# Attention scores of a decoder layer: three partial passes packed into two full ones and a pair of half-height ones

## The reference

```python
# q: (2, 16 heads, 512 queries, 96), k and v: (2, 4 groups, 1536 keys, 96); 4 heads share a group
scores = jnp.einsum('bkgqd,bksd->bkgqs', q, k) * scale          # scale = 1/sqrt(96)
attn = jax.nn.softmax(scores.astype(jnp.float32), axis=-1)
out = jnp.einsum('bkgqs,bksd->bkgqd', attn, v)
```

## Time and profile before

| | us |
|---|---|
| median of 3 runs | 3467.85 (3467.83 to 3468.65) |
| time of the profiled execution | 3465.8 |
| its span, first to last instruction | 3464.5 |
| PE busy, whole span | 3015.0 (87%) |
| attention, first score matmul to last value matmul | 1661.3 to 2306.1 |
| mean granted TensorE clock, whole span | 0.917 of full speed |

### The profile page before, as it was taken

One profiled execution on the slowest core, in us unless ns is written; L12 is line 12 of the kernel. 1 busy time (PEld: TensorE's weight loads), 2 busy tenths in 40 slices (PEclk: granted clock), 3 DMA queues, 4 the chain that ended last, 5 costly groups with the idle time before them and its releaser, 6 DMA issues. The chain is left out here.

```text
span 3464.5 us, 37038 instructions
## 1 busy us (share of the span) xinstructions
PE 3015.0 (87%) x12731; PEld 2191.7 (63%) x12731; DVE 2160.8 (62%) x1655; ACT 1502.2 (43%) x2400; POOL 1391.3 (40%) x796
## 2 busy tenths in 40 slices
PE   8994567776774799998999999979899999999996
PEld 7861222222231478886788888867688888888884
DVE  5557799999999565401777777764734324324326
ACT  4446355555554443311688888862322112112111
POOL 0003899999999331000688888850100000000001
PEclk9985788887885799999899999989999999999998
DMA  3225865655554474322111111134211101111101
GB/s 139 88 75 209 240 162 125 155 145 149 127 136 114 165 260 166 105 76 92 33 33 51 33 33 37 33 113 147 68 46 53 58 34 53 52 39 54 49 18 61
DMA packets 159386, 331.29 MB, mean 96 GB/s; under 512 B 28221, under 2 KB 40253, under 8 KB 157789
## 3 DMA queue, kind: packets, MB, share of 16 engines
q1 hardware_dynamic: 141694, 320.11, 30.5%
q10 hardware_dynamic: 17568, 9.66, 0.9%
HBM read 257.03 MB, written 72.68 MB: 95 GB/s over the span
## 5 line engine op out<-in xcount | busy, mean ns | idle before, releaser
L731 POOL TENSOR_TENSOR scan_dbx<-scan_u,scan_b_bc 128x1024 f32<-128x1024 f32 x256 | 595.0, 2357 | 25.0 <-DMA scan_u<-u 21.8
L1545 POOL TENSOR_TENSOR at_p_lo<-at_p,at_p_hi 128x512 fp32r<-128x512 f32 x384 | 516.7, 1352 | 148.3 <-ACT at_p_hi L1451 137.2
L918 POOL TENSOR_TENSOR ff_y<-ff_y,ff_rstd 128x512 f32<-128x512 f32 x14 | 24.9, 1806 | 1123.0 <-DVE ff_rstd L907 1123.0
L682 ACT ACTIVATE scan_ps_a<-scan_dt,scan_a_neg 128x512 f32<-128x512 f32 (+1 forms) x512 | 331.7, 680 | 289.8 <-DVE scan_g L694 271.0
L705 DVE TENSOR_TENSOR_SCAN scan_ps_a<-scan_ps_a,scan_dbx 128x1024 f32<-128x1024 f32 x192 | 433.1, 2282 | 7.0 <-ACT scan_ps_a L684 7.0
L792 PE MATMUL scan_ps_y<-scan_g,scan_sel 128*32 128x512 f32 x1024 | 176.2, 765 | 220.8 <-DVE scan_g L694 216.3
L1490 DVE TENSOR_REDUCE at_neg_max<-at_ps_mx 128x1 fp32r<-128x1536 f32 x132 | 232.0, 1758 | 154.4 <-PE at_ps_mx L1565 143.3
L1965 DVE TENSOR_TENSOR ff_hf<-ff_sg,ff_ps_u 128x1024 f32<-128x1024 f32 x28 | 34.2, 1221 | 388.4 <-PE ff_ps_u L98 388.4
L1448 ACT ACTIVATE at_p<-at_ps_s 128x512 f32<-128x512 f32 x384 | 227.9, 593 | 105.2 <-PE at_ps_s L1582 84.2
L1451 ACT ACTIVATE at_p_hi<-at_p 128x512 fp32r<-128x512 f32 x384 | 242.8, 632 | 12.3
L772 PE MATMUL scan_ps_x<-scan_x,scan_wz 128*128 128x512 f32 x448 | 230.0, 661 | 13.5 <-DMA scan_wz<-in_w_in 13.5
(11 more groups left out here) (260 smaller groups left out, 7255.7 us busy)
## 6 DMA issues: line engine op xcount, KB each, us to landing
scan_dt<-dt SPq DMA_DIRECT2D x128, 256.0 KB, 4.6
scan_u<-u SPq DMA_DIRECT2D x128, 256.0 KB, 7.6
ff_w<-in_w SPq DMA_DIRECT2D x56, 512.0 KB, 4.2
mid_w<-in_w_out SPq DMA_DIRECT2D x32, 512.0 KB, 4.7
ff_w<-in_w SPq DMA_DIRECT2D x56, 256.0 KB, 2.6
ff_wo_wo<-in_w_o SPq DMA_DIRECT2D x32, 384.0 KB, 3.1
in_w<-in_w_in SPq DMA_DIRECT2D x18, 512.0 KB, 3.7
xc<-xc SPq DMA_DIRECT2D x16, 512.0 KB, 2.8
```

The source lines that it names most:

```text
L682: nc.scalar.activation(at[:, h * L + h:(h + 1) * L], dt[it % 2][:, c, h:L], ACT.Exp, scale=a_neg[:, it % IT, e:e + 1]).then_inc(a_ready, 1)
L731: nc.gpsimd.tensor_tensor(dbx[n % SL][:].rearrange("p (h l) -> p h l", h=2), u[it % 2][:, c:c + 2], b_bc[:, b, k // 2].unsqueeze(1).to_bro ...
L1545: nc.gpsimd.tensor_tensor(p_lo[t % NSL][:], p[t % NSL][:], f32(p_hi[t % NSL][:]), ALU.subtract).then_inc(p_lo_done, 1)
```

## The change

The three score passes of a tile have 97 + 96 + 96 = 289 rows. The change packs them otherwise: a first pass of 128 rows (`ka`, `qa`: 96 rows high by high, and the first 32 rows of the keys' rest by the queries' high part), a second of 128 rows (`kb`, `qb`: the other 64 rows of the keys' rest, and 64 rows of high by the queries' rest), and a third of 33 rows (`kc`, `qc`: the last 32 rows of high by rest, and the row of maxima). The 33 rows stand twice in `kc` and `qc`, at partitions 0 and 64, and of two key tiles the even one uses rows 0 to 32, the odd one rows 64 to 96.

So that two tiles' third passes stand together, PE works by pairs: two full passes of tile 2j, two of tile 2j+1, then both third passes, then (in j = 5) the transposes, then two tiles of `values`, then, in j = 0 to 3, a maximum of the next head. ACT does two exponentials, then two high parts.

The parts are put in place by DMAs from SBUF to SBUF, which SP issues: five for each head (`stack_q`) and five for each group (`stack_k`). The row of maxima is copied twice: by ACT to partition 96 and by DVE to partition 32 (`row`), for which DVE also copies the column of maxima (`second_column`). The maxima of head 0 use two sets of banks in turn (`ps_first`); keys and values have semaphores of their own; the values of non-existing tiles and the maxima of the non-existing 33rd head are gone.

```diff
-    SPLIT_AT = ((1, 4), (1, 7), (1, 10), (2, 1), (2, 4), (2, 9))
+    SPLIT_AT = ((1, 2), (1, 3), (1, 4), (2, 0), (2, 1), (2, 3))
...
+            def stack_q(hd):
+                s, e = hd % 2, hd % NQ
+                sp.wait_ge(q_hi_done, hd + 1)
+                sp.dma_start(f32(qb[e][0:64]), f32(qa[e][32:96])).then_inc(q_stacked[s], 16)
+                sp.dma_start(f32(qa[e][96:128]), f32(qa[e][0:32])).then_inc(q_stacked[s], 16)
+                sp.wait_ge(q_lo_done, hd + 1)
+                sp.dma_start(f32(qb[e][64:128]), f32(q_lo[s][0:64])).then_inc(q_stacked[s], 16)
+                sp.dma_start(f32(qc[e][0:32]), f32(q_lo[s][64:96])).then_inc(q_stacked[s], 16)
+                sp.dma_start(f32(qc[e][64:96]), f32(q_lo[s][64:96])).then_inc(q_stacked[s], 16)
...
+            for hd in range(NHD):
+                w, g = divmod(hd, G)
+                for j in range(ST // 2):
+                    exponential(hd, 2 * j)
+                    exponential(hd, 2 * j + 1)
+                    if j == 5 and hd + 1 < NHD:
+                        row(hd + 1)
+                    head(hd, 2 * j)
+                    head(hd, 2 * j + 1)
+                    if j == 1 and hd + 2 < NHD:
+                        queries(hd + 2)
+                    if (g, j) in SPLIT_AT and w + 1 < NW:
+                        split_kv(w + 1, SPLIT_AT.index((g, j)))
...
+            queries(0)
+            split_k(0)
             maximum(0, 0)
-            queries(0, 0)
-            maximum(0, 1)
-            split_k(0, 0)
+            maximum(0, 1, ps_first)
             maximum(0, 2)
-            split_v(0, 0)
-            maximum(0, 3)
-            queries(1, 1)
-            heads(dve, body)
-            reciprocals(NHD, 0)
-            divide(NHD, 0)
+            maximum(0, 3, ps_first)
+            second_column(0)
+            row(0)
+            split_v(0)
+            queries(1)
+            for hd in range(NHD):
+                w, g = divmod(hd, G)
+                more = hd + 1 < NHD
+                if more:
+                    maximum(hd + 1, 0)
+                    maximum(hd + 1, 1)
+                if hd:
+                    reciprocals(hd - 1)
+                if more:
+                    maximum(hd + 1, 2)
+                if hd:
+                    divide(hd - 1)
+                if more:
+                    maximum(hd + 1, 3)
+                    second_column(hd + 1)
+                if hd + 2 < NHD:
+                    queries(hd + 2)
+                if more:
+                    row(hd + 1)
+                if g == 1 and w + 1 < NW:
+                    split_k(w + 1)
+                if g == 2 and w + 1 < NW:
+                    split_v(w + 1)
...
-            def scores(hd, t, e, s):
-                pe.wait_ge(exp_done, ST * hd + t + 1)
-                c = slice(t * P, (t + 1) * P)
-                nc.tensor.matmul(ps_s[t % 2][:], k_hi[s][:, c], q_hi[e][:], start=True, stop=False)
-                nc.tensor.matmul(ps_s[t % 2][:], k_hi[s][0:HD, c], q_lo[e][:], start=False, stop=False)
-                nc.tensor.matmul(ps_s[t % 2][:], k_lo[s][:, c], q_hi[e][0:HD], start=False, stop=True).then_inc(s_mm, 1)
+            def scores(hd, j):
+                s, e = hd // G % 2, hd % NQ
+                for t in (2 * j, 2 * j + 1):
+                    n = ST * hd + t
+                    if n >= 2:
+                        pe.wait_ge(exp_done, n - 1)
+                    c = slice(t * P, (t + 1) * P)
+                    nc.tensor.matmul(ps_s[t % 2], ka[s][:, c], qa[e][:], start=True, stop=False)
+                    nc.tensor.matmul(ps_s[t % 2], kb[s][:, c], qb[e][:], start=False, stop=False)
+                if j == 0:
+                    pe.wait_ge(row_done, hd + 1)
+                    pe.wait_ge(row_copied, hd + 1)
+                for t in (2 * j, 2 * j + 1):
+                    c, r = slice(t * P, (t + 1) * P), slice(64 * (t % 2), 64 * (t % 2) + NB1 + 1)
+                    nc.tensor.matmul(ps_s[t % 2], kc[s][r, c], qc[e][r], start=False, stop=True).then_inc(s_mm, 1)
...
-                    if t in (0, 2, 5, 7):
-                        nw = w + 1 if g == G - 1 else w
-                        maximum(hd + 1, nw, (g + 1) % NQ, 1 - s if g == G - 1 else s, (0, 2, 5, 7).index(t))
-                    if t == 10:
-                        transposes(hd + 1)
...
+            for hd in range(NHD):
+                w, g = divmod(hd, G)
+                pe.wait_ge(q_stacked[hd % 2], 16 * STACKS * (hd // 2 + 1))
+                if g == 0:
+                    pe.wait_ge(k_stacked[w % 2], 16 * STACKS * (w // 2 + 1))
+                for j in range(ST // 2):
+                    scores(hd, j)
+                    if j == 5 and hd + 1 < NHD:
+                        transposes(hd + 1)
+                    for n in range(ST * hd + 2 * j - LAG, ST * hd + 2 * j - LAG + 2):
+                        if n >= 0:
+                            values(n)
+                    if j < QT and hd + 1 < NHD:
+                        maximum(hd + 1, j)
```

More of the change, by code:

```diff
@@ L1422, in _, with split_kv @@
+            store(NHD - 1)
+            for s in range(2):
+                sp.wait_ge(on_st[s], 16 * NHD // 2)
         @block.scalar
         def _(act):
-            def split_kv(w, s, part):
-                act.wait_ge(kv_ld, 32 * (w + 1))
+            def split_kv(w, part):
+                s = w % 2
                 if part < 3:
                     c = slice(part * L, (part + 1) * L)
-                    nc.scalar.activation(k_hi[s][0:HD, c], k[:, c], ACT.Copy).then_inc(kv_hi_done, 1)
+                    act.wait_ge(k_ld, 16 * (w + 1))
+                    nc.scalar.activation(ka[s][0:HD, c], k[:, c], ACT.Copy).then_inc(k_hi_done, 1)
@@ L1461, in _, with queries @@
-            act.sem_inc(exp_done, 2)
-            queries(0, 0)
-            for part in range(6):
-                split_kv(0, 0, part)
-            queries(1, 1)
+                    act.wait_ge(v_ld, 16 * (w + 1))
+                    nc.scalar.activation(v_hi[s][:, c, 0:HD], v[:, c], ACT.Copy).then_inc(v_hi_done, 1)
+            def queries(hd):
+                act.wait_ge(q_ld[hd % 2], 16 * (hd // 2 + 1))
+                nc.scalar.activation(qa[hd % NQ][0:HD], q[hd % 2][:], ACT.Copy).then_inc(q_hi_done, 1)
@@ new lines, in row, with exponential, head @@
+            def row(hd):
+                act.wait_ge(t_mm, hd + 1)
+                nc.scalar.activation(qc[hd % NQ][HD:HD + 1], ps_t[HD:HD + 1], ACT.Copy).then_inc(row_done, 1)
+            def exponential(hd, t):
+                n = ST * hd + t
+                act.wait_ge(s_mm, n + 1)
+                if n >= NSL:
+                    act.wait_ge(p_lo_done, n - NSL + 1)
+                nc.scalar.activation(p[t % NSL][:], ps_s[t % 2], ACT.Exp, scale=SCALE).then_inc(exp_done, 1)
+            def head(hd, t):
+                n = ST * hd + t
+                act.wait_ge(exp_done, n + 1)
+                if n >= NSL:
+                    act.wait_ge(pv_mm, n - NSL + 1)
+                nc.scalar.activation(p_hi[t % NSL][:], p[t % NSL][:], ACT.Copy).then_inc(p_hi_done, 1)
@@ L1466, in _ @@
+            for part in range(3):
+                split_kv(0, part)
+            queries(0)
+            for part in range(3, 6):
+                act.wait_ge(pool_set, POOL_SET)
+                split_kv(0, part)
             act.wait_ge(id_ld, 16)
             nc.scalar.activation(ident_r[:], ident[:], ACT.Copy).then_inc(id_done, 1)
-            row(0, 0)
-            act.wait_ge(before_done, 1)
-            heads(act, body)
+            queries(1)
[13 more added lines that the diff above has]
+                        split_kv(w + 1, SPLIT_AT.index((g, j)))
@@ L1557, in _, with maximum @@
+            nc.gpsimd.memset(v_lo[1][:, :, HD:P].bitcast(F32), 0.0).then_inc(pool_set, 1)
+            for n in range(ST * NHD):
+                pool.wait_ge(p_hi_done, n + 1)
+                if n >= NSL:
+                    pool.wait_ge(pv_mm, n - NSL + 1)
+                nc.gpsimd.tensor_tensor(p_lo[n % NSL][:], p[n % NSL][:], f32(p_hi[n % NSL][:]),
+                                        ALU.subtract).then_inc(p_lo_done, 1)
         @block.tensor
         def _(pe):
-            def maximum(hd, w, e, s, i):
+            def maximum(hd, i, at=ps_mx, behind=0):
@@ L1610, in _ @@
             for i in range(QT):
-                maximum(0, 0, 0, 0, i)
+                maximum(0, i, ps_first if i % 2 else ps_mx, 1)
             pe.wait_ge(id_done, 1)
@@ L1614, in _ @@
             pe.wait_ge(pool_set, POOL_SET)
-            nc.tensor.matmul(ps_o[1][:], v_hi[1][:, 0], p_hi[NSL - 1][:], start=True, stop=False).then_inc(before_done, 1)
-            pe.sem_inc(pv_mm, NSL - LAG)
             transposes(0)
-            heads(pe, body)
-            for t in range(ST - LAG, ST):
-                pe.wait_ge(p_lo_done, NSL + ST * (NHD - 1) + t + 1)
-                values(1, t, 1)
+            for hd in range(NHD):
+                w, g = divmod(hd, G)
```

(4 more changed lines are left out.)

250 lines of the change are left out of this document (113 added, 137 removed).

## The result

The changed kernel takes 3507.45 us (median of 4 runs, 3505.52 to 3509.02), the kernel before 3468.25 us (4 runs, 3467.83 to 3470.77). The ratio is 1.0111, with a 95% interval of 1.0094 to 1.0129: 39 us slower. The forecast was 3513, slower, with a range of 3455 to 3530. The profiled execution of the changed kernel took 3505.52 us around a span of 3504.2.

A forecast was written before the change was run, and what follows sets the result against it. PE's own instructions were taken to bound the kernel. Heads 1 to 30 add 52.8 us, start and end take 8.1 off: +44.7, so the profiled 3465.8 becomes 3510.5 and the median 3513; range 3455 to 3530.

The forecast's parts named there:

- The switch: PE going into half-height matmuls and back costs, as in the scan phase, 0.42 us a pair; chance 0.56.
- s: What a pair of key tiles costs PE beyond its five slots of 0.233 us; taken as 0.42, bounds 0.33 and 0.51.
- The full queueing of the second load: Upper bound at a pair: the second half's weight load waits wholly behind the first's, up to another 0.11 us.
- The wait for DVE: PE waits to write maximum 3 until DVE frees `ps_mx`: 1.37 - 2s, so 0.53 us, plus 0.11 for the load.
- A steady head: Each of heads 1 to 30 takes 21.71 us instead of 19.95, together +52.8 us.
- Start and end: One-time terms: start -6.1, head 0 -1.0, head 31 -2.0, tail +1.0; together -8.1 us.
- head 31 and the tail: Last head without maxima or transposes: -2.0 us; PE's longer wait for POOL's last rest: +1.0.
- the cold start: What head 0 takes beyond a steady head: 3.2 us, carried over from the kernel before.
- The cover: Work of ACT, POOL, DVE copies and SP's DMA issues, costed at nothing because it finishes before PE needs it.
- A free switch: Rival: no switch cost, halves side by side, s = 0; 3458 us, faster by 0.28%; chance 0.22.
- halves one after the other: Rival: no switch cost but serial halves, s = 0.233; 3488 us; chance 0.15 together with a cheap switch.
- a dearer switch: Rival: a drain of full depth with cold loads at each pair, s = 0.69; 3544 us; chance 0.07.

The follow-up runs named there:

- halves_apart: recip_late with each tile's third pass right behind its own two full passes, so PE goes into a half and back twice a pair; 3606.70 us, ratio 1.0400.
- recip_late: Changed kernel with DVE's reciprocal moved behind maximum 2 and the divides behind the row copy; 3489.46 us, ratio 1.0063 to the kernel before.
- same_half: Changed kernel with both third passes of a pair in rows 0 to 32, the same half of the array; 3536.10 us, ratio 1.0197 to before.
- full_rows: Changed kernel with every third pass through the full array at 97 rows, unused rows zero, no halves; 3493.46 us, ratio 1.0074 to before.
- full_rows_recip_late: Changed kernel with both edits, 97-row third passes and the reciprocal behind maximum 2; 3462.72 us, ratio 0.9986 to before.
- full_rows_q_first: full_rows_recip_late with head 0's queries loaded between the keys and the values at the start; 3464.35 us, ratio 0.9990 to before.

## Why the prediction held

**The switch, the main term.** "With the same price into the halves, s = 0.40" plus 0.02: measured 0.39 from the starts in the timeline, 0.37 from halves_apart against recip_late (24.53 - 20.91 = 3.62 us a head, less six slots). The gap of 0.09 us in each direction and the unhidden load of 0.11 us, read from cuts by columns, hold for cuts by rows: in the changed kernel 0.20 us stand together on the way out, and in same_half they come apart, the second half 0.10 us late behind the first, the full one 0.09 behind that. The full queueing of the second load (s = 0.51) is ruled out by the merged load row of 0.19 us and the two starts 3 ns apart. The Trainium skill (TensorEngine Tiling (Array Packing), Key Properties) has the rule that changing the mode drains the array; halves_apart agrees: 192 round trips more cost 117 us, of which 45 are the slots that no longer overlap (192 x 0.233). What the runs show is the empty 0.09 us and the late load at each change; that the array drains in between is the reading of it.

**The wait for DVE.** Foretold 0.53 + 0.11 us, in front of maximum 3, in 31 heads. Measured 0.64 + 0.11: with s at 0.39 the formula 1.37 - 2s gives 0.59. Shown by recip_late, which takes it away; a head gets only 0.53 us shorter, for a wait of 0.23 us comes up in front of the transposes.

**A steady head.** Foretold 21.71, measured 21.44. With s = 0.39 the formula gives 18.55 + 2.34 + 0.59 + 0.11 = 21.59; what remains, 0.15, is the slot, 0.228 rather than 0.233 us in some stretches (2003.37 to 2004.05 is 0.68 for three). This is the largest error of the sum: 52.8 us foretold for heads 1 to 30, 44.0 measured.

**Start and end.** Foretold -8.1. In the profiled executions the start, from DVE's first memset of the phase to PE's first score matmul, went from 27.50 us (1633.76 to 1661.26) to 23.49 (1635.50 to 1658.99), so -4.0 instead of -6.1. The rows of the changed kernel show what was missed:

```profile
1635.50 0.38 DVE L1555 MEMSET at_neg_max<- 128x388 f32 x1 [18.70 <-PEq L1039]
...
1642.84 1.67 ACT L1452 ACTIVATE at_ka<-at_k 96x512 fp32r<-96x512 f32 x3 [10.81 <-DMA at_k<-k]
1646.60 0.63 ACT L1460 ACTIVATE at_qa<-at_q 96x512 fp32r<-96x512 f32 x1 [2.10 <-DMA at_q<-q]
...
1658.99 0.77 PE L1640 MATMUL at_ps<-at_qa,at_ka 128*128 128x512 f32 x1 [1.24 <-DMA at_kb<-at_k_lo]
```

The first queries, now issued behind keys and values, came 2.1 us late, and the last of the stacking DMAs held PE another 1.24 us. The prediction named the second as a risk and gave it no time: it had 0.43 us for each of the ten issues, and in this trace they stand some 0.6 apart or more (1647.31 to 1654.55). The first it missed, but most of it belongs to this one execution: in the profiles of the five experiments that load in the same order, ACT waits 0.48 to 0.67 us for these queries, and the start takes 21.5 to 22.4 us instead of 23.49. From the first score matmul to the last value matmul the time rose by 42.5 us (644.4 to 686.9), of which heads 1 to 30 are 44.0 (19.97 and 21.44 us each); head 31 and the tail are -1.8, foretold -1.0, and head 0 is +0.3, foretold -1.0. For head 0 the prediction carried the cold start, which it put at 3.2 us, over unchanged. It isn't unchanged: it was 2.5 us before (22.49 less a steady 19.97) and is some 4 now (22.77, where 66 slots, the transposes, six pairs and the wait for DVE are 18.7), for the granted clock stays at 0.50 nearly twice as long (see the last section). The phases ahead ended 1.7 us later in this execution and those behind took 0.5 less, with nothing changed in them. So 1.7 - 4.0 + 42.5 - 0.5 = 39.7 us of span, where 44.7 was foretold. The total is nearer than the steady heads alone (8.8 too much), because start and head 0, 3.4 us too low together, cancel a part of their error; that part is luck.

**The cover.** ACT, POOL and SP were costed at nothing, and no wait of a steady head names them but one: PE's first load of values waits for POOL's rest in 39 pairs, 10.3 us in all on PEld. It costs nothing: the row after the halves has the same idle time, 0.24 to 0.25 us, whether POOL or "issue" is named.

**The rivals.** A free switch is out (s = 0.39), halves one after the other are out (same_half), a dearer switch is out. The free one would have been the only way to be faster, and even then, by the wait for DVE, by little; full_rows, which has no switch, is 26 us over the kernel before and shows that wait at 0.94 us a head. The prediction's cover for DVE's column copy, 0.1 to 0.6 us, holds in the changed kernel (0.17) and fails in four of the experiments (0.63 to 1.25).

## What to carry over

Going into a row-cut array and back costs 0.39 us here, whether one half-height matmul, two side by side or two in a row stand inside, and running two matmuls of 512 columns side by side gives back 0.23 us. By these numbers packing pays only where two or more such pairs stand inside one round trip; that is an estimate from them, and no run here has two pairs in one. Before packing matmuls, look in the trace of the kernel at hand for any place where the array changes shape, and read the distances between starts there; cuts by columns foretold cuts by rows to 0.03 us. And when work of a bound engine is regrouped, redo the distances at which it comes back to a shared buffer: eight slots fewer between the second and the fourth maximum turned a hidden reciprocal into 0.75 us a head. Moving it away let a smaller wait behind it come up, 0.23 us a head, so look for the next one too.

## What the runs showed of the hardware

**The clock comes up later with half-height matmuls in the stream.** Just before head 0 the granted clock is 0.50 (1.2 GHz) in every run. Windows of 1 us, counted from the first score matmul, show when it is at 1.00 (2.4 GHz) throughout, and the distance from that matmul to the next head's first shows what head 0 costs:

| kernel | third passes | first window at 1.00, us after the first score matmul | head 0, us |
|---|---|---|---|
| before | none (three passes of 96 or 97 rows) | 6 | 22.49 |
| full_rows | 97 rows, full array | 6 | 19.68 |
| full_rows_recip_late | 97 rows, full array | 6 | 19.68 |
| full_rows_q_first | 97 rows, full array | 6 | 19.67 |
| changed kernel | two halves side by side | 11 | 22.77 |
| recip_late | two halves side by side | 12 | 23.33 |
| same_half | two in one half, in a row | 16 | 26.13 |
| halves_apart | one half at a time | 19 | 29.79 |

Heads 1 to 30 of full_rows are 0.24 us shorter than those of the changed kernel, its head 0 is 3.1 us shorter. No run here separates the gaps at the change of mode from the half-height matmuls themselves as the reason.

**A small DVE copy is held by POOL.** The column copy (128 x 4) takes 170 ns in the changed kernel, every time; in recip_late the same instruction has a median of 980 ns. The timeline of recip_late shows it standing under POOL's subtraction:

```profile
2010.20 3.06 POOL L1607 TENSOR_TENSOR at_p_lo<-at_p,at_p_hi 128x512 fp32r<-128x512 f32 x2 [1.09 <-ACT at_p_hi L1479]
...
2010.54 0.98 DVE L1540 CAST at_neg_max<-at_neg_max 128x4 fp32r<-128x4 f32 x1
2011.43 0.68 DVE L1522 TENSOR_TENSOR at_q_lo<-at_q,at_qa 96x512 fp32r<-96x512 f32 x1
```

One such subtraction takes 1.29 us as a rule, so the first of the two ends near 2011.49, and the copy ends at 2011.52. The experiments put the copy at several places under that subtraction, and it always ends about 0.03 us after it:

| kernel | POOL's subtraction still has, when the copy starts | the copy takes |
|---|---|---|
| changed kernel, same_half, halves_apart | POOL is idle | 0.17 us |
| full_rows_recip_late, full_rows_q_first | 0.60 us | 0.63 us |
| recip_late | 0.95 us | 0.98 us |
| full_rows | 1.22 us | 1.25 us |

In the kernels of the last three lines PE's transposes wait for it, which is the 0.23 to 0.25 us a head named above. The other way round, POOL's two subtractions, which meet DVE's subtraction of the queries, take 3.06 us here instead of twice 1.29. The same subtraction on DVE took 1.316 us on the mean in the kernel before, where it begins 0.5 us after one of POOL's, and 0.689 in the changed one, where it begins 0.04 us ahead of POOL's. The Trainium skill (SBUF — State Buffer, SBUF: two separate sides) describes a port pair that one of the two engines locks for a whole instruction; these rows agree with it. No edit was made for this question alone.
